# LSTM with attention: scores in groups of 64 keys, and the hidden part of the output made turned

## The chip, the cores and the metric

The kernel runs on one core of one Trainium2 chip. The metric is device time in microseconds (us). The kernel before took 5734.92 us (median of 3 runs, 5734.32 to 5736.79).

## The reference

The whole program is a small decoder of two layers: a linear recurrence, an LSTM with attention, a mixture of experts, an RWKV-7 scan, cross attention and a second mixture. The change touches the LSTM with attention, which runs 512 steps one after the other for 4 sequences, with 256 features and 512 source positions (keys) per sequence:

```python
def attend(h):
    q = h @ Wq.T
    scores = jnp.einsum('bc,bsc->bs', q, context)
    alpha = jax.nn.softmax(scores, axis=-1)
    ctx = jnp.einsum('bs,bsc->bc', alpha, context)
    return jnp.tanh(jnp.concatenate([ctx, h], axis=-1) @ Wout.T + b_out)

def step(carry, x_t):
    h, c, attn = carry
    inp = jnp.concatenate([x_t, attn], axis=-1)
    gates = inp @ W_ih.T + b_ih + h @ W_hh.T + b_hh
    i, f, g, o = jnp.split(gates, 4, axis=-1)
    c = jax.nn.sigmoid(f) * c + jax.nn.sigmoid(i) * jnp.tanh(g)
    h = jax.nn.sigmoid(o) * jnp.tanh(c)
    attn_out = attend(h)
    return (h, c, attn_out), attn_out
```

Every step needs the attention output of the step before, so the steps can't overlap.

## The kernel before

`prepare_phase` (L169) computes once, before the steps: the input's share of the gates (`xg_rows` in DRAM), the context folded with Wq (`keys`) and with the context half of Wout (`values`, bias included). With these a step needs only products of h with `keys`, of the softmax weights with `values`, and of h with `w_out_h`.

`attention_lstm_phase` (L663) holds the steps. Its loop body has two steps and runs 256 times. Each engine has its own program, written out by hand, and the engines meet at semaphores. All matmuls are fp32; the profile shows two records for each. TensorE is used in strips: its 128 output partitions are four strips of 32, and four matmuls, each with one strip, run side by side. In most places a strip is a sequence (batch) b; in `turn`, `select` and the gates it is one of the four quarters of a row of outputs.

One step, in PE's order (L922 to L958):

- `scores(c, k)` (L852): chunk c of 128 keys, half k of h. For each b, a window of 4 columns of `hid` is the stationary operand. h of b stands in column PAD + SPACE*b and the rest is zero, so the window that starts c columns earlier puts the scores of chunk c in row c of strip b. `part` 0 holds chunks 0 and 1, `part` 1 chunks 2 and 3, each a bank region of 128 columns. Half k = 0 can start when h[0] is there, k = 1 when h[1] is.
- DVE takes the maximum of a part (L1053), ACT the exp (L990). Parts have maxima of their own, and the differences are put right at the end by the `shrink` factors (L995, L1065 to L1077).
- `turn(part)` (L878): a matmul with columns of the identity as moving operand turns the exps so that keys lie on partitions; ACT copies them to `alpha` (L993).
- `hidden_part` (L862): h times `w_out_h`, h stationary (17 columns) and the weights moving, 6 matmuls of 128 or 64 columns, into rows of the `ctx` banks that the context leaves free. `hidden_sel` in `masks` picks those rows later.
- `half_hid(0, 0)`: part of the next gates. Then `context(c, n)` (L870): the alphas of chunk c times `values`, output piece n of three (128, 64 and 64 columns), each row of a strip a chunk. `turn(1)` lies among them.
- `select(o)` (L886): after ACT and DVE have copied the context to `out_row`, a matmul with `sel_scaled` (4 moving columns) adds up the rows of each sequence with their softmax factors, and the hidden rows with factor 1, and turns the result to feature-major. ACT takes tanh of it to `attn` (L1004).
- `gates`: `o_gate_x_hid`, then `half_attn` of both halves and `o_gate_attn`. DVE and ACT compute the cell and h from them (L1011 to L1030), while PE starts the next step's `half_x`.

`by_batch` picks every SPACE-th column, the four sequences; ROWS (13) is the number of stationary columns in the gates' matmuls.

Of the kernel before, what the change touches and what calls it, by code (L numbers as in the profile page):

```python
# [2 lines left out]

# [139 lines left out]
SPACE = 4  # L143
ROWS = SPACE * (BATCH - 1) + 1
PAD = SPACE
PARTS = 2
XROWS = TOK + UNROLL * BATCH


SEL, OWN_PART, HIDDEN_SEL, PLACE = 0, BATCH, BATCH + SC, 2 * BATCH + SC  # L150
MASKS = PLACE + ROWS
# [17 lines left out]
def prepare_phase(nc, d, g, xg_dram, w_attn, w_hid, w_out_h, keys, values, ident, masks):  # L169
# [5 lines left out]
    with Scope(nc) as s:  # L175
# [27 lines left out]
        KV_LOADS, GATES_LOADS = 4, 8  # L203
# [47 lines left out]
        def _(sp):  # L251
# [13 lines left out]
            sp.dma_start(ident[:, :], d["ident"]).then_inc(gates_loaded, 16)  # L265
# [397 lines left out]
def attention_lstm_phase(nc, d, g):  # L663
# [14 lines left out]
    with Scope(nc) as s:  # L678
# [5 lines left out]
        ident = s.sb("lstm_ident", [P, P])  # L684
        masks = s.sb("lstm_masks", [P, MASKS])

        prepare_phase(nc, d, g, xg_dram, w_attn, w_hid, w_out_h, keys, values, ident, masks)

        sel_batch = masks[:, SEL:SEL + BATCH]
        own_part = masks[:, OWN_PART:OWN_PART + SC]  # L690
        hidden_sel = masks[:, HIDDEN_SEL:HIDDEN_SEL + BATCH]
        place = masks[:, PLACE:PLACE + ROWS]
        with Scope(nc) as q:
# [11 lines left out]
            expo = q.sb("lstm_expo", [P, PARTS, P])  # L705
            alpha = q.sb("lstm_alpha", [P, BATCH, SC, 2 * SPACE - 1])
            spread_max = q.sb("lstm_spread_max", [P, 2 * (STRIP + 4)])
            spread_total = q.sb("lstm_spread_total", [P, 2 * (STRIP + 4)])
            neg_max_all = q.sb("lstm_neg_max_all", [P, 1])
            shrink = q.sb("lstm_shrink", [P, SC])  # L710
            weighed = q.sb("lstm_weighed", [P, SC])
            total_sum = q.sb("lstm_total_sum", [P, 1])
            own_terms = q.sb("lstm_own_terms", [P, SC])
# [10 lines left out]
            ctx_half = [0, 1, 1]  # L724
# [60 lines left out]
            def alpha_rows(part):  # L785
                return alpha[:, :, 2 * part:2 * part + 2, SPACE - 1]

            def turned_rows(part):
                return turned_ps[part].rearrange("p (b r) -> p b r", r=2)
# [19 lines left out]
            def _(pe):  # L809
# [42 lines left out]
                def scores(c, k):  # L852

                    part, n = c // 2, c % 2
                    for b in range(BATCH):
                        lo = PAD + SPACE * b - c
                        mm = pe.matmul(part_rows(score_ps[part], b), hid[:, k, lo:lo + SPACE],  # L857
                                       keys[:, k, b * SRC + c * P:b * SRC + (c + 1) * P],
                                       start=(n == 0 and k == 0), stop=(n == 1 and k == KC - 1))
                    return mm  # L860

                def hidden_part():  # L862

                    for k in range(KC):
                        for n, cols in enumerate(ctx_cols):
                            j = KC * k + ctx_half[n]
                            pe.matmul(ctx_ps[n][j * STRIP:j * STRIP + PAD + ROWS, :], hid[:, k, 0:PAD + ROWS],
                                      w_out_h[:, k, cols], start=True, stop=False)

                def context(c, n):  # L870

                    for b in range(BATCH):
                        mm = pe.matmul(part_rows(ctx_ps[n], b), alpha[:, b, c, SPACE - 1 - c:2 * SPACE - 1 - c],  # L873
                                       values[:, b * SC + c, ctx_cols[n]],
                                       start=(c == 0 and b % KC != ctx_half[n]), stop=(c == SC - 1))
# [1766 lines left out]
```

## Time and profile before

| | |
|---|---|
| median of 3 runs | 5734.92 us |
| profiled execution | 5734.24 us |
| its span | 5732.5 us |
| TensorE (PE) busy | 5209.2 us, 91% |
| VectorE (DVE) busy | 3553.1 us, 62% |
| ScalarE (ACT) busy | 1985.4 us, 35% |
| granted TensorE clock, mean | 0.968 |

Durations are read from the profiled execution. The span is the time from its first to its last instruction. The busy time of an engine is the time in which at least one of its instructions runs, so four matmuls side by side count once. The duration of one matmul record contains the fill and drain of the array; how closely matmuls follow each other is read from the starts. "PEld" is TensorE's loading of stationary operands. Each LSTM step looks like the others, so one step of the timeline stands for all.

### The profile page before, as it was taken

What the parts mean: (1) busy time and instruction counts of PE and PEld (TensorE: products, weight loads), DVE (VectorE), ACT (ScalarE), POOL (GpSimd) and SP (SyncE); (2) the same over time, 40 slices, a digit from 0 to 9 for tenths busy, and PEclk for the clock granted to TensorE, in tenths of its full rate; (3) what the DMA queues carried; (4) which work ended last, traced back from release to release, by engine and by line L of the source; (5) the groups of instructions that cost most, each with busy time, mean ns of one, the idle gap of its engine ahead of it and who ended that gap; (6) DMA issues with size and microseconds to landing.
All of it is one profiled execution on the core that took longest, in us unless ns stands there. A gap on an engine that the chain in (4) does not pass through costs nothing. (4 is left out here: it accounts for less than half of the span.)

```text
span 5732.5 us, 382651 instructions
## 1 busy us (share of the span) xinstructions
PE 5209.2 (91%) x171240; PEld 3824.2 (67%) x171240; DVE 3553.1 (62%) x15410; ACT 1985.4 (35%) x7977; POOL 345.7 (6%) x795
## 2 busy tenths in 40 slices
PE   9899999999999999999999999998688879797989
PEld 4677877877878778778778778776444434443433
DVE  5455555555555555555555555554798999999931
ACT  2244444444444444444444444442222222223221
POOL 0000000000000000000000000000111211212100
PEclk9999999999999999999999999999799889898999
DMA  2000000000000000000000000002111101010111
GB/s 99 35 2 2 2 2 2 2 2 2 2 2 2 2 2 2 2 2 2 2 2 2 2 2 2 2 2 86 45 54 39 44 16 54 25 54 25 57 36 54
DMA packets 45677, 111.60 MB, mean 19 GB/s; under 512 B 8192, under 2 KB 10240, under 8 KB 45072
## 3 DMA queue, kind: packets, MB, share of 16 engines
q1 hardware_dynamic: 44144, 109.39, 6.2%
q10 hardware_dynamic: 1440, 1.06, 0.1%
q8 instruction: 48, 0.79, 0.1%
q14 instruction: 45, 0.37, 0.0%
HBM read 99.90 MB, written 10.52 MB: 19 GB/s over the span
## 5 line engine op out<-in xcount | busy, mean ns | idle before, releaser
L857 PE MATMUL lstm_part_ps<-lstm_keys,lstm_hid 128*4 128x128 f32 x32768 | 1025.9, 273 | 207.1 <-DVE lstm_hid L1029 207.1
L857 PEld LDWEIGHTS lstm_part_ps<-lstm_keys,lstm_hid 128*4 128x4 f32 x32768 | 770.6, 86 | 431.5 <-DVE lstm_hid L1029 417.2
L873 PE MATMUL lstm_ctx_ps<-lstm_values,lstm_alpha 128*4 128x128 f32 (+1 forms) x49152 | 1041.2, 237 | 0.3 <-issue 0.3
L873 PEld LDWEIGHTS lstm_ctx_ps<-lstm_values,lstm_alpha 128*4 128x4 f32 x49152 | 905.6, 86 | 64.8 <-issue 0.5
L1053 DVE TENSOR_REDUCE lstm_neg_max<-lstm_part_ps 128x1 f32<-128x128 f32 x1024 | 299.2, 292 | 678.9 <-PE lstm_part_ps L857 678.9
L1011 DVE STREAM_TRANSPOSE lstm_gates<-lstm_half_ps 128x96 f32<-128x96 f32 x1026 | 290.6, 283 | 567.6 <-PE lstm_half_ps L816 543.8
L990 ACT ACTIVATE lstm_expo<-lstm_part_ps,lstm_neg_max 128x128 f32<-128x128 f32 x1024 | 376.4, 368 | 649.0 <-DVE lstm_neg_max L1053 649.0
L816 PE MATMUL lstm_half_ps<-lstm_w_hid,lstm_hid 128*13 128x96 f32 x16384 | 564.0, 245 | 0.0
L816 PE MATMUL lstm_half_ps<-lstm_w_attn,lstm_attn 128*13 128x96 f32 x16448 | 435.0, 246 | 1.6 <-issue 1.6
L2087 ACT ACTIVATE mix_gated<-mix_gate_ps 115x512 f32<-115x512 f32 (+2 forms) x200 | 112.6, 563 | 776.2 <-PE mix_gate_ps L1815 776.1
L816 PEld LDWEIGHTS lstm_half_ps<-lstm_w_hid,lstm_hid 128*13 128x13 f32 x16384 | 367.4, 94 | 0.0
L979 ACT ACTIVATE lstm_cell<-lstm_gates 128x12 f32<-128x12 f32 x1024 | 224.6, 219 | 411.1 <-DVE lstm_gates L1011 411.1
L1815 PE MATMUL mix_gate_ps<-xT,mix_ring 128*115 128x512 f32 (+3 forms) x800 | 363.8, 578 | 0.0
L1824 PE MATMUL mix_up_ps<-mix_xw,mix_ring 128*115 128x512 f32 (+2 forms) x704 | 320.7, 579 | 46.2 <-DVE mix_weighted L2391 37.4
L1844 PE MATMUL mix_down_ps<-mix_weighted,mix_ring 115*128 115x512 f32 (+3 forms) x800 | 358.4, 571 | 1.1 <-DVE mix_weighted L2391 1.0
L1094 POOL TENSOR_TENSOR xT<-xT,lstm_attn 128x8 f32 x512 | 105.2, 206 | 3636.2 <-ACT lstm_attn L1004 3636.2
L816 PEld LDWEIGHTS lstm_half_ps<-lstm_w_attn,lstm_attn 128*13 128x13 f32 x16448 | 302.6, 93 | 19.3 <-issue 2.0
L816 PE MATMUL lstm_half_ps<-lstm_xg,lstm_masks 128*13 128x96 f32 x8224 | 306.6, 250 | 8.7 <-DMA lstm_xg<-xg_rows 8.7
L993 ACT COPY lstm_alpha<-lstm_part_ps 128x8 f32<-128x8 f32 x1024 | 177.9, 174 | 377.7 <-PE lstm_part_ps L882 377.7
L2364 DVE TENSOR_TENSOR rw_terms<-rw_state,rw_sc 128x384 f32<-128x384 f32 x512 | 299.7, 585 | 6.7
L987 ACT ACTIVATE lstm_tanh_c<-lstm_cell 128x4 f32<-128x4 f32 x1024 | 210.7, 206 | 196.6 <-DVE lstm_cell L1022 154.6
L1029 DVE SCALAR_TENSOR_TENSOR lstm_hid<-lstm_o_col,lstm_tanh_c 128x4 f32<-128x4 f32 x1024 | 170.8, 167 | 174.0 <-ACT lstm_tanh_c L987 139.2
(324 smaller groups left out, 8196.2 us busy)
## 6 DMA issues: line engine op xcount, KB each, us to landing
mix_ring<-in_sm_chunks SPq DMA_DIRECT2D x120, 358.0 KB, 3.0
mix_ring<-in_mix_chunks SPq DMA_DIRECT2D x80, 384.0 KB, 3.1
lstm_xg<-xg_rows SPq DMA_DIRECT2D x514, 16.0 KB
xg_rows<-rec_lam SPq DMA_DIRECT2D x16, 512.0 KB, 2.6
xT<-in_xT SPq DMA_DIRECT2D x4, 512.0 KB, 8.7
ctxT<-in_ctxT SPq DMA_DIRECT2D x1, 2048.0 KB, 14.5
out_xT<-xT SPq DMA_DIRECT2D x4, 512.0 KB, 3.8
lstm_w_x<-in_lstm_w_x SPq DMA_DIRECT2D x1, 1024.0 KB, 17.2
```

The costliest lines, as they stand in the source:

```text
L816: mm = pe.matmul(ps[j * STRIP:j * STRIP + ROWS, :], rows, w[:, j * HID + cols.start:j * HID + cols.stop], start=start, stop=stop)
L857: mm = pe.matmul(part_rows(score_ps[part], b), hid[:, k, lo:lo + SPACE], keys[:, k, b * SRC + c * P:b * SRC + (c + 1) * P], start=(n == 0 ...
L873: mm = pe.matmul(part_rows(ctx_ps[n], b), alpha[:, b, c, SPACE - 1 - c:2 * SPACE - 1 - c], values[:, b * SC + c, ctx_cols[n]], start=(c == ...
L979: act.activation(cell[:, k, 0:GATES - 1, :], by_batch(turned), ACT.Tanh).then_inc(half_tanh[k], 1)
L987: act.activation(tanh_c[:, k, :], cell[:, k, GATES - 1, :], ACT.Tanh, scale=0.5).then_inc(c_tanh[k], 1)
L990: act.activation(expo[:, part, :], score_ps[part], ACT.Exp, bias=neg_max[:, part:part + 1]).then_inc(exp_ready, 1)
L1011: dve.transpose(gates[:, k, :], half_ps[k]).then_inc(half_turned[k], 1)
L1053: dve.tensor_reduce(neg_max[:, part:part + 1], score_ps[part], AX_X, ALU.max, negate=True)\
L1815: mm = pe.matmul(gate_ps[0:m, 0:width], ring[:, at, k * e:k * e + m], token_block(x, i)[:, k, :], start=(k == 0), stop=(k == KC - 1))
L1824: mm = pe.matmul(up_ps[0:m, 0:width], ring[:, at, lo:lo + m], xw[:, k, 0:width] if x.weighted(n) else token_block(x, i)[:, k, :], start=(k ...
L1844: mm = pe.matmul(down_ps[:, o_, 0:width], ring[0:m, gn % RING, lo + o_ * P:lo + (o_ + 1) * P], gw[0:m, gn % 2, 0:width], start=(n == 0), s ...
L2364: dve.tensor_tensor(terms[:, :, :, :], before.unsqueeze(1).to_broadcast([P, 3, HALF, HD]), sc[:, parity, UNIT_KEY:RECV + 1, t, :].unsqueez ...
```

## The change

SPACE becomes 8 and the 512 keys of a sequence are scored in 8 groups of 64 (`SUBS`, `SUB`). A part is now 4 groups: 4 rows of a strip, 64 columns. A window of `hid` has 8 columns instead of 4 and starts up to 7 columns earlier. The number of score matmuls doubles, from 32 to 64 a step, each with 64 moving columns instead of 128. The maximum, the exp and the sum of the exps run over 64 columns per part instead of 128.

`turn` writes 16 columns instead of 8: both halves of a 128-key chunk are brought back together, group 2*pair to partitions 0 to 63 and group 2*pair + 1 to partitions 64 to 127. Its moving operand is no longer the identity but 16 columns of `masks`, side by side, with zeros elsewhere. `alpha` takes two rows for each chunk, and the context's window moves by 2 a chunk. Softmax factors exist for 8 groups instead of 4.

`hidden_part` has operands exchanged: 32 columns of `w_out_h` are stationary, and four elements of h, 8 apart, are moving. There are 16 matmuls of 4 columns instead of 6 of 64 or 128. They write straight into `attn_ps`, and `select` accumulates on them (start=False). `hidden_sel` goes, so `sel_scaled` is a plain multiplication. `attn_ps[1]` gets a PSUM bank of its own, and `turned_ps[0]` moves to a context bank. ROWS becomes 25, by which the gates' matmuls have 25 stationary columns.

```diff
-SPACE = 4
+SUB = P // 2
+SUBS = SRC // SUB
+SPACE = SUBS
 ROWS = SPACE * (BATCH - 1) + 1
 PAD = SPACE
 PARTS = 2
+PART_SUBS = SUBS // PARTS
+TURNED = BATCH * PART_SUBS
...
-            expo = q.sb("lstm_expo", [P, PARTS, P])
-            alpha = q.sb("lstm_alpha", [P, BATCH, SC, 2 * SPACE - 1])
+            expo = q.sb("lstm_expo", [P, PARTS, SUB])
+            alpha = q.sb("lstm_alpha", [P, BATCH, SC, 2 * SPACE])
...
-            attn_ps = [part_ps[o][:, P:P + BATCH] for o in range(KC)]
-            score_ps = [part_ps[n][:, 0:P] for n in range(PARTS)]
-            turned_ps = [part_ps[n][:, 2 * P:2 * P + 2 * BATCH] for n in range(PARTS)]
+            attn_bank = q.ps("lstm_attn1_ps", [P, NB])
+            attn_ps = [part_ps[0][:, P:P + BATCH], attn_bank[:, 0:BATCH]]
+            score_ps = [part_ps[n][:, 0:SUB] for n in range(PARTS)]
+            turned_ps = [bank[:, 2 * P:2 * P + TURNED] for bank in (ctx_bank[KC], part_ps[1])]
...
             def alpha_rows(part):
-                return alpha[:, :, 2 * part:2 * part + 2, SPACE - 1]
+                return alpha[:, :, 2 * part:2 * part + 2, SPACE - 1:SPACE + 1]
...
                 def scores(c, k):
 
-                    part, n = c // 2, c % 2
+                    part, n = divmod(c, PART_SUBS)
                     for b in range(BATCH):
                         lo = PAD + SPACE * b - c
                         mm = pe.matmul(part_rows(score_ps[part], b), hid[:, k, lo:lo + SPACE],
-                                       keys[:, k, b * SRC + c * P:b * SRC + (c + 1) * P],
-                                       start=(n == 0 and k == 0), stop=(n == 1 and k == KC - 1))
+                                       keys[:, k, b * SRC + c * SUB:b * SRC + (c + 1) * SUB],
+                                       start=(n == 0 and k == 0), stop=(n == PART_SUBS - 1 and k == KC - 1))
                     return mm
 
+                def part_scores(part, k):
+
+                    for n in range(PART_SUBS):
+                        mm = scores(part * PART_SUBS + n, k)
+                    return mm
+
                 def hidden_part():
 
-                    for k in range(KC):
-                        for n, cols in enumerate(ctx_cols):
-                            j = KC * k + ctx_half[n]
-                            pe.matmul(ctx_ps[n][j * STRIP:j * STRIP + PAD + ROWS, :], hid[:, k, 0:PAD + ROWS],
-                                      w_out_h[:, k, cols], start=True, stop=False)
+                    for o in range(KC):
+                        for k in range(KC):
+                            for j in range(QUARTERS):
+                                lo = o * P + j * STRIP
+                                pe.matmul(attn_ps[o][j * STRIP:(j + 1) * STRIP, :], w_out_h[:, k, lo:lo + STRIP],
+                                          by_batch(hid[:, k, PAD:]), start=(k == 0), stop=False)
...
                 def turn(part):
 
-                    part_columns = ident[:, :].rearrange("p (b r) -> p b r", r=STRIP)[:, :, 2 * part:2 * part + 2]
                     for j in range(QUARTERS):
-                        mm = pe.matmul(turned_ps[part][j * STRIP:(j + 1) * STRIP, :], expo[:, part, j * STRIP:(j + 1) * STRIP],
-                                       part_columns, start=True, stop=True)
+                        half, lo = j // 2, j % 2 * STRIP
+                        col = TURN + (2 * part + half) * TURNED
+                        mm = pe.matmul(turned_ps[part][j * STRIP:(j + 1) * STRIP, :], expo[:, part, lo:lo + STRIP],
+                                       masks[:, col:col + TURNED], start=True, stop=True)
                     mm.then_inc(alpha_turned, 1)
...
                         mm = pe.matmul(attn_ps[o][j * STRIP:(j + 1) * STRIP, :], out_row[:, lo:lo + STRIP], sel_scaled[:, :],
-                                       start=True, stop=True)
+                                       start=False, stop=True)
...
                         pe.wait_ge(h_ready[0], t + 1)
-                        for c in (0, 1):
-                            scores(c, 0)
+                        part_scores(0, 0)
                         pe.wait_ge(h_ready[1], t + 1)
-                        scores(0, 1)
-                        scores(1, 1).then_inc(scores_ready, 1)
-                        for c in (2, 3):
-                            scores(c, 0)
-                        scores(2, 1)
-                        scores(3, 1).then_inc(scores_ready, 1)
+                        part_scores(0, 1).then_inc(scores_ready, 1)
+                        part_scores(1, 0)
+                        part_scores(1, 1).then_inc(scores_ready, 1)
...
-                        dve.scalar_tensor_tensor(out=sel_scaled[:, :], in0=sel_shrunk[:, :], scalar=inverse[:, 0:1],
-                                                 in1=hidden_sel, op0=ALU.mult, op1=ALU.add).then_inc(sel_ready, 1)
+                        dve.tensor_scalar(sel_scaled[:, :], sel_shrunk[:, :], inverse[:, 0:1], None, ALU.mult).then_inc(sel_ready, 1)
```

## Rows read from the trace of the kernel before

**Rows 1.** The page's first part: busy time, share of the span, instructions.

```profile
PE 5209.2 (91%) x171240; PEld 3824.2 (67%) x171240; DVE 3553.1 (62%) x15410; ACT 1985.4 (35%) x7977; POOL 345.7 (6%) x795
```

**Rows 2.** Windows: length, busy time and records of each engine, clock, DMA.

```profile
190.00:3800.00 3610.00, 3408.20 (x160264) 2882.02 (x160268) 1991.56 (x11376) 1475.47 (x6924) 101.54 (x494) 1.00 0.01 2
```

**Rows 3.** Timeline of one LSTM step: start us, length us, engine, line, operation.

```profile
2001.82 2.00 PE L857 MATMUL lstm_part_ps<-lstm_keys,lstm_hid 128*4 128x128 f32 x64 [0.41 <-DVE lstm_hid L1029]
...
2002.33 1.20 PEld L857 LDWEIGHTS lstm_part_ps<-lstm_keys,lstm_hid 128*4 128x4 f32 x48 [0.18 <-DVE lstm_hid L1029]
2003.02 0.29 DVE L1053 TENSOR_REDUCE lstm_neg_max<-lstm_part_ps 128x1 f32<-128x128 f32 x1 [0.74 <-PE lstm_part_ps L857]
2003.34 0.37 ACT L990 ACTIVATE lstm_expo<-lstm_part_ps,lstm_neg_max 128x128 f32<-128x128 f32 x1 [1.27 <-DVE lstm_neg_max L1053]
...
2003.76 0.25 PE L882 MATMUL lstm_part_ps<-lstm_ident,lstm_expo 128*32 128x8 f32 x8
...
2003.85 0.42 PE L867 MATMUL lstm_ctx_ps<-lstm_w_out_h,lstm_hid 128*17 128x128 f32 x12
2003.89 0.29 DVE L1053 TENSOR_REDUCE lstm_neg_max<-lstm_part_ps 128x1 f32<-128x128 f32 x1 [0.58 <-PE lstm_part_ps L857]
...
2004.06 0.37 PE L816 MATMUL lstm_half_ps<-lstm_w_hid,lstm_hid 128*13 128x96 f32 x8
2004.08 0.17 ACT L993 COPY lstm_alpha<-lstm_part_ps 128x8 f32<-128x8 f32 x1 [0.37 <-PE lstm_part_ps L882]
2004.22 0.37 ACT L990 ACTIVATE lstm_expo<-lstm_part_ps,lstm_neg_max 128x128 f32<-128x128 f32 x1
...
2004.30 0.51 PE L873 MATMUL lstm_ctx_ps<-lstm_values,lstm_alpha 128*4 128x128 f32 x16
...
2004.64 0.25 PE L882 MATMUL lstm_part_ps<-lstm_ident,lstm_expo 128*32 128x8 f32 x8
...
2004.72 1.62 PE L873 MATMUL lstm_ctx_ps<-lstm_values,lstm_alpha 128*4 128x64 f32 x80
...
2005.90 0.22 DVE L1077 SCALAR_TENSOR_TENSOR lstm_sel_scaled<-lstm_sel_shrunk,lstm_inverse,lstm_masks 128x4 f32<-128x4 f32 x1
2005.96 0.27 ACT L998 COPY lstm_out_row<-lstm_ctx_ps 128x128 f32<-128x128 f32 x1 [0.64 <-PE lstm_ctx_ps L873]
...
2006.15 0.51 PE L816 MATMUL lstm_half_ps<-lstm_w_hid,lstm_hid 128*13 128x96 f32 x16
...
2006.71 0.22 PE L890 MATMUL lstm_part_ps<-lstm_sel_scaled,lstm_out_row 128*32 128x4 f32 x8
...
2006.77 0.29 PE L816 MATMUL lstm_ctx_ps<-lstm_xg,lstm_masks 128*13 128x64 f32 x8
...
2007.10 0.84 PE L816 MATMUL lstm_half_ps<-lstm_w_attn,lstm_attn 128*13 128x96 f32 x32
...
2007.76 0.41 PE L816 MATMUL lstm_ctx_ps<-lstm_w_attn,lstm_attn 128*13 128x64 f32 x16
...
2009.11 0.62 PE L857 MATMUL lstm_part_ps<-lstm_keys,lstm_hid 128*4 128x128 f32 x16 [0.41 <-DVE lstm_hid L1029]
```

**Rows 4.** Waits of 1000 to 3500 us: total us, times, longest.

```profile
PEld lstm_part_ps L882 <- ACT lstm_expo L990: 79.4, 343, 0.2
```

**Rows 5.** Groups by line and form, 1000 to 3500 us: busy us, mean ns.

```profile
L1053 DVE TENSOR_REDUCE lstm_neg_max<-lstm_part_ps 128x1 f32<-128x128 f32 x686 | 200.5, 292 | 454.0 <-PE lstm_part_ps L857 454.0
...
L1061 DVE TENSOR_REDUCE lstm_total<-lstm_expo 128x2 f32<-128x256 f32 x343 | 144.0, 420 | 0.0
...
L998 ACT COPY lstm_out_row<-lstm_ctx_ps 128x128 f32<-128x128 f32 x343 | 91.4, 267 | 220.5 <-PE lstm_ctx_ps L873 220.5
...
L1000 ACT COPY lstm_out_row<-lstm_ctx_ps 128x64 f32<-128x64 f32 x343 | 73.0, 213 | 0.0
```

**Rows 6.** Instruction queue: packets, MB, share; whole span, then 190 to 3800 us.

```profile
q8 instruction: 48, 0.79, 0.1%
...
q8 instruction: 5, 0.08, 0.0%
```

More of the change, by code:

```diff
@@ L2 @@
 from contextlib import ExitStack
+import itertools
 import numpy as np
@@ L166, in sigmoid_columns, with prepare_phase @@
     return [halves_of(ap)[:, :, :, 0:2 * STRIP], quarters(ap)[:, :, KC * HALF_W:]]
-def prepare_phase(nc, d, g, xg_dram, w_attn, w_hid, w_out_h, keys, values, ident, masks):
+def prepare_phase(nc, d, g, xg_dram, w_attn, w_hid, w_out_h, keys, values, masks):
     QT = NB // QUARTERS
@@ L683, in attention_lstm_phase @@
         values = s.sb("lstm_values", [P, BATCH * SC, DIM])
-        ident = s.sb("lstm_ident", [P, P])
         masks = s.sb("lstm_masks", [P, MASKS])
-        prepare_phase(nc, d, g, xg_dram, w_attn, w_hid, w_out_h, keys, values, ident, masks)
+        prepare_phase(nc, d, g, xg_dram, w_attn, w_hid, w_out_h, keys, values, masks)
         sel_batch = masks[:, SEL:SEL + BATCH]
-        own_part = masks[:, OWN_PART:OWN_PART + SC]
-        hidden_sel = masks[:, HIDDEN_SEL:HIDDEN_SEL + BATCH]
+        own_part = masks[:, OWN_PART:OWN_PART + SUBS]
         place = masks[:, PLACE:PLACE + ROWS]
@@ L785, in alpha_rows @@
             def alpha_rows(part):
[L786 removed]
+                return alpha[:, :, 2 * part:2 * part + 2, SPACE - 1:SPACE + 1]
             def turned_rows(part):
[L789 removed]
+                return turned_ps[part].rearrange("p (b c h) -> p b c h", b=BATCH, h=2)
             @block.sync
@@ L870, in context @@
                 def context(c, n):
                     for b in range(BATCH):
-                        mm = pe.matmul(part_rows(ctx_ps[n], b), alpha[:, b, c, SPACE - 1 - c:2 * SPACE - 1 - c],
+                        mm = pe.matmul(part_rows(ctx_ps[n], b), alpha[:, b, c, SPACE - 1 - 2 * c:2 * SPACE - 1 - 2 * c],
                                        values[:, b * SC + c, ctx_cols[n]],
-                                       start=(c == 0 and b % KC != ctx_half[n]), stop=(c == SC - 1))
+                                       start=(c == 0), stop=(c == SC - 1))
@@ L1030, in new_hidden @@
                                              in1=tanh_c[:, k, :], op0=ALU.add, op1=ALU.mult).then_inc(h_ready[k], 1)
-                for ps in (*half_ps, *part_ps, *ctx_bank):
+                for ps in (*half_ps, *part_ps, *ctx_bank, attn_bank):
                     dve.memset(ps[:, :], 0.0)
@@ L2617, in laid_out @@
         masks[b * STRIP:b * STRIP + SPACE, SEL + b] = 1
-        for j in range(QUARTERS):
-            masks[j * STRIP + PAD + SPACE * b, HIDDEN_SEL + b] = 1
         masks[b, PLACE + SPACE * b] = 1
-    for c in range(SC):
+    for c in range(SUBS):
         masks[np.arange(QUARTERS) * STRIP + c, OWN_PART + c] = 1
+    for b, c in itertools.product(range(BATCH), range(SUBS)):
+        part, n = divmod(c, PART_SUBS)
+        pair, half = divmod(n, 2)
+        masks[b * STRIP + c, TURN + (2 * part + half) * TURNED + b * PART_SUBS + 2 * pair + half] = 1
     d["lstm_masks"] = masks
```

23 lines of the change are left out of this document (11 added, 12 removed).

## The prediction

> **What bounds the kernel now.** I read the busy shares first: TensorE (PE) is busy 91% of the span, DVE 62%, ACT 35% [rows 1]. Only the LSTM phase is edited, so next the view by stages: from 190 to 3800 us the clock is granted in full and PE is busy 3408 of 3610 us, 94% [rows 2]. The printed chain of waits follows only the phases behind the loop, so the bound has to be read from one step's timeline [rows 3]. Its first score matmul starts at 2001.82 and the next step's at 2009.11, so a step takes 7.29 us, and 512 of them 3732 us. Below, 3.76 means 2003.76.
>
> PE is in three states in a step. (a) From 1.82 it does 64 score records (32 fp32 matmuls, two records each). They are four concurrent streams, one per strip of 32 output partitions, so I count in rounds of four records. Part 0 is complete at 3.02, where DVE takes its maximum; ACT's exp runs 3.34 to 3.71, and PE's `turn(0)` starts at 3.76. PE ran out of scores before that: the wait of its weight loads at L882 for this exp is 79.4 us over 343 steps, 0.23 a step [rows 4]. (b) From 3.76 to 4.30 PE does `turn(0)`, `hidden_part`, `half_hid(0,0)` and then waits a little for `alpha`, which ACT copies out at 4.08 to 4.25. (c) From 4.30 to the end of the gates PE's rows follow each other without a gap; what it needs comes earlier than it asks: `sel_scaled` is done at 6.12 and `out_row` of piece 0 at 6.23, while the second `select` begins at 6.71. Behind the gates the cell update runs on DVE and ACT, untouched but for strides. So the step is one serial ring, and in (c) any shift of PE shifts the end by as much.
>
> **Prices in rounds** [rows 3]. 64 columns: L816 into ctx goes 6.77 to 7.10, 24 records, 0.33/6 = 0.055; I use 0.056. 96 columns: 7.10 to 7.76, 8 rounds, 0.0825. 128 columns: L873 x80 starts 4.72, its follower 6.15; 1.43 less 14 rounds of 0.056 leaves 0.108 for each of 6; I use 0.109. `select` (4 contiguous moving columns, 32-wide weights): 6.71 to 6.77 for two rounds, 0.03 each. `turn` (8 moving columns, taken in pairs 32 elements apart): 4.64 to 4.72, nearer 0.085 for two rounds with both turns read. So small matmuls with a broken-up moving operand cost about 0.085 a pair of rounds, contiguous ones 0.06.
> The Trainium skill (TensorE: Matmul & The Clock Gate, "Wait — 56ns, not 53.3ns?") says that start-to-start never drops under about 25 ns however small the matmul is. By that alone the 84 more records of a step would cost 2.1 us, some 1075 us in all. The trace disagrees where the records go to four strips: L882's eight records at 4.64 have all begun when the next line's begins at 4.72, some 10 ns each.
>
> **Part by part.**
> 1. *Scores in eight groups of 64 keys.* Records per step 64 to 128, each half as wide. From h[1] (weight load at 2.33) 12 rounds of 0.109 = 1.31 become 24 of 0.056 = 1.34: PE is free at 3.67 instead of 3.64. Before h[1]: 8 rounds of 0.056 = 0.45 in place of 0.44, and 0.51 are there (1.82 to 2.33), free. Part 0's last round starts 0.05 later and its matmul is 0.05 shorter, so part 0 is ready at 3.03, part 1's maximum starts at 3.93 instead of 3.89.
> 2. *Maximum over 64 columns.* 292 ns for 128 and 420 for 2x128 [rows 5]: 1.0 ns a column, 0.228 instead of 0.292, each part.
> 3. *Exp over 64 columns.* Copies by ACT take 267 ns for 128 columns, 213 for 64 [rows 5]: 0.054 less. Exp 0 ends at 3.71 + 0.01 - 0.064 - 0.054 = 3.60; `turn(0)` could start 0.05 later, 3.65, but PE is free at 3.67. It starts at 3.67, 0.09 earlier. What was PE's wait is now PE's own work. Exp 1 ends at 4.59 + 0.034 - 0.118 = 4.51.
> 4. *`turn`* has 16 contiguous moving columns from `masks` instead of 8 in pairs. Bounds are 0.06 and 0.085; I take 0.06, since the length is still far under 64 columns and it is contiguous like `select`'s. It is two rounds, so 0.025 saved, twice a step. ACT's copy grows by 8 columns, 0.007.
> 5. *`hidden_part`* turned: 6 matmuls become 16, 12 records 32, in 8 rounds. The moving operand is four elements of h, now 8 apart. Before: 3.85 to 4.06, 0.21. After, 4 pairs of rounds: 0.24 as `select`, 0.34 as `turn`, 0.45 at the price of 64 columns. I take 0.34, the nearest row with a broken-up moving operand. The Trainium skill (SBUF — State Buffer, "Door 1: The DMA port swizzle", its paragraph on cachelines) has a penalty for each access that crosses to a new 16-byte line; four elements 32 bytes apart are four lines, `turn`'s old pattern also four. `select`'s price against `turn`'s old one agrees with it, the rule points to 0.34 rather than 0.24.
> 6. *Where the context starts.* PE: 3.67 + 0.06 + 0.34 + `half_hid(0,0)` 0.165 = 4.23. `alpha[0]`: 0.54 from `turn(0)` to the context before (3.76 to 4.30), less 0.025 and more 0.007, gives 4.19. PE decides: 4.23 against 4.30. Up to `turn(1)` lie 2 x 0.109 + 2 x 0.056 = 0.33: 4.56, and exp 1 + 0.05 is 4.56 too, against 4.64. `turn(1)` gives 0.025 more. All of stage (c) is 0.095 earlier.
> 7. *`select` accumulates on the hidden part in PSUM, `sel_scaled` is a plain scaling.* Count and form of `select` stay, the DVE instruction is about as long (0.22) and has 0.5 us of slack; nothing. Own terms, shrink, weights over 8 instead of 4 columns: some ns each on a DVE chain that moves up by 0.08 with exp 1, hidden behind the contexts. Sum of exps: 0.13 shorter, also hidden. Weight loads of 8, 25 instead of 4, 13 columns: `turn` and `select` load 32 in rounds of 0.03, so every round of 0.056 or more covers them.
> 8. *Outside the loop*: one DMA less (the identity), larger masks, one more bank zeroed: 0 to 1 us once.
>
> Sum: 512 x 0.095 = 48.6 us less, 0.5 more. The profiled execution took 5734.24 us for a span of 5732.5; the median is 5734.92, 0.7 above, and I count from it: 5734.9 + 0.5 - 48.6 = 5686.8 us. Own range of this case: `turn` not cheaper (context at 4.255, 0.046 a step, 24 us) up to hidden at 0.24 (exp 1 decides; 0.109 a step, 56 us): 5680 to 5712.
>
> **Rivals.**
> *A. The turned hidden part costs as much as 64 columns or more* (0.056 a round). Its 0.45 put the context at 4.345 and `turn(1)` at 4.675; with 0.025 back the step is 0.01 longer: +5 us, 5740, no change, and slower if the price is higher still. For it: single elements 32 bytes apart are in no row. Against: the old `turn` broke its operand as often at less. Chance 0.09.
> *B. PE's instruction supply becomes the bound, slower.* No row shows rounds of 56 ns for long: 64-column runs last 6 rounds; the densest long stretch, 4.64 to 7.76, has 184 records in 3.12 us, 17.0 ns each, where the new scores ask for 14. If 17 is what the sequencer can feed, 96 records take 1.63, PE is free at 3.96, 0.29 later than in my sum, and the step is 0.2 longer: +100 us, 5837. It decides from about 15 ns a record. Against it: the 24 records from 6.77 and those just ahead of them come at 14 and less, and the 17.0 is fully explained by column counts. Chance 0.09.
> *C. The loop's code outgrows what PE holds.* From 190 to 3800 us the instruction queue moved 5 packets [rows 6]: the loop of two steps (1296 PE records) is fetched once and stays. The new one has 1632. If it doesn't stay, at least one packet is exposed at each of 256 jumps back. The whole span's 48 packets took 0.1% of 16 engines' time [rows 6], 92 us or 1.9 each, roughly: +490 us, 6180. Chance 0.04.
> The Trainium skill (Runtime: NRT & Kernel Launch, "Instruction fetch mechanics") gives PE room for 2048 instructions, by which 1632 stay; it also says that a jump outside two pages refetches, and five pages that are fetched once disagree with that.
> *D. The score part is better than summed* (the maximum or exp shrink more, rounds under 56 ns): 5672 or less. Chance 0.05.
>
> **How the numbers follow.** Forecast 0.73, A 0.09, B 0.09, C 0.04, D 0.05. The measurement tells 0.2%, 11.5 us, from no change. Faster: forecast and D and a little of A, 0.79; same 0.09; slower: B, C and a little of A, 0.12. The range 5670 to 5728 leaves out B, C, most of A and part of D.
>
> **What would show it.** A step of 7.195 us; PE's wait at L882 for exp 0 gone; 64-column score rounds of 56 ns; `turn(0)` 0.09 earlier; maxima near 228 ns and exps near 314; the 32 hidden records in about 0.34 us; no gap between `half_hid(0,0)` and the first context. Wrong: rounds of the scores over 60 ns (B), hidden records over 14 ns apart (A), instruction packets spread over the loop (C), or ACT's exp not shrinking, which would bring the wait at L882 back.

## The result, and the profile after

The changed kernel takes 7878.84 us (median of 4 runs, 7876.14 to 7893.32) against 5734.77 us: 1.3744 times as long, 95% interval 1.3727 to 1.3762. The forecast was 5687 us, with 5670 to 5728 as its range. Rival C, to which I gave 0.04, is what happened, and at more than four times the price I had put on it (2144 us over the kernel before, where I had 490).

The page of the changed kernel, its parts 1, 3 and 5:

```profile
PE 5708.2 (72%) x214248; PEld 4507.2 (57%) x214248; DVE 3418.8 (43%) x15411; ACT 1929.8 (24%) x7977; POOL 346.1 (4%) x795
...
q8 instruction: 1193, 19.55, 1.2%
...
L860 PE MATMUL lstm_part_ps<-lstm_keys,lstm_hid 128*8 128x64 f32 x65536 | 1370.2, 248 | 1083.5 <-issue 913.4
...
L1060 DVE TENSOR_REDUCE lstm_neg_max<-lstm_part_ps 128x1 f32<-128x64 f32 x1024 | 230.1, 225 | 1914.8 <-PE lstm_part_ps L860 1914.8
...
L997 ACT ACTIVATE lstm_expo<-lstm_part_ps,lstm_neg_max 128x64 f32<-128x64 f32 x1024 | 321.2, 314 | 1662.9 <-DVE lstm_neg_max L1060 1662.9
```

Two rows are as forecast: the maximum takes 225 ns (228 forecast, 292 in [rows 5]) and the exp 314 ns (314 forecast). Two are not: PE falls from 91% busy [rows 1] to 72%, and the instruction queue moves 1193 packets where it moved 48 [rows 6]. In front of the score matmuls PE is idle for 913 us with "issue" as the cause, which means that nothing in the profile was being waited for. On the page of the kernel before, the scores' line has 207.1 us of idle time ahead of it, all of it put down to DVE's `lstm_hid` and none to "issue".

PE's own timeline shows both faces of the changed loop (start, length; in brackets the idle time before and its cause):

```profile
2015.57 2.04 PE L860 MATMUL lstm_part_ps<-lstm_keys,lstm_hid 128*8 128x64 f32 x128 [0.39 <-DVE lstm_hid L1036]
2017.42 0.24 PE L893 MATMUL lstm_ctx_ps<-lstm_masks,lstm_expo 128*32 128x16 f32 x8
2017.48 0.29 PE L877 MATMUL lstm_part_ps<-lstm_hid,lstm_w_out_h 128*32 128x4 f32 x16
...
2017.80 0.38 PE L819 MATMUL lstm_half_ps<-lstm_w_hid,lstm_hid 128*25 128x96 f32 x7
2018.00 0.52 PE L883 MATMUL lstm_ctx_ps<-lstm_values,lstm_alpha 128*8 128x128 f32 x16
2018.34 0.23 PE L893 MATMUL lstm_part_ps<-lstm_masks,lstm_expo 128*32 128x16 f32 x8
2018.39 1.62 PE L883 MATMUL lstm_ctx_ps<-lstm_values,lstm_alpha 128*8 128x64 f32 x80
...
2020.78 0.85 PE L819 MATMUL lstm_half_ps<-lstm_w_attn,lstm_attn 128*25 128x96 f32 x32
...
2021.80 0.60 PE L819 MATMUL lstm_half_ps<-lstm_xg,lstm_masks 128*25 128x96 f32 x16
2026.66 1.03 PE L860 MATMUL lstm_part_ps<-lstm_keys,lstm_hid 128*8 128x64 f32 x29 [4.26 <-issue]
2030.19 2.10 PE L860 MATMUL lstm_part_ps<-lstm_keys,lstm_hid 128*8 128x64 f32 x72 [2.51 <-issue]
```

The step from 2015.57 is undisturbed: the gates' attention part begins 5.21 us after the first score matmul, where the kernel before needs 5.28 (7.10 - 1.82, [rows 3]). Then the loop jumps back and PE stands still for 4.26 us with nothing to wait for, does 29 records, and stands still for 2.51 us more. So the change does what it was meant to do where it can run, and something that isn't in any of its instructions costs 2171 us (7878.8 less the 5707.7 us of e2 below, whose loop is the same).

Over the loop, windows of the changed kernel and of e2 (length; busy time and records of PE, PEld, DVE, ACT, POOL; granted clock; DMA):

```profile
230.00:6000.00 5770.00, 3942.98 (x204558) 3588.71 (x204554) 1886.71 (x11535) 1441.67 (x7020) 102.45 (x501) 0.88 0.02 5
```

```profile
230.00:3800.00 3570.00, 3375.47 (x201560) 3114.85 (x201556) 1835.77 (x11362) 1438.19 (x6917) 100.81 (x494) 1.00 0.01 2
```

Brought to the same number of records (x 1.015), e2 needs 3623 us, 3426 of them busy. The changed kernel is busy 517 us longer and idle 1630 us longer. In its loop the granted clock is 0.88 in the mean, a mixture of stretches at 2.4 and at 1.2 GHz; in e2, which issues the same instructions without the pauses, it is 1.00. So the lower clock comes with the pauses, and it costs at most a quarter of the loss: 517 of 2147 us, in which longer busy time from work cut up by pauses is contained too.

### The profile page after: what moved, and what is told of

The parts are those of the page before. It is cut to its first block and busy times, and to the rows that moved or that the text cites. A ratio compares the mean times of both kernels' runs of the same rounds, so it can differ in the third digit from the quotient of the medians.

```text
span 7878.1 us, 468667 instructions
## 1 busy us (share of the span) xinstructions
PE 5708.2 (72%) x214248; PEld 4507.2 (57%) x214248; DVE 3418.8 (43%) x15411; ACT 1929.8 (24%) x7977; POOL 346.1 (4%) x795
## 3 DMA queue, kind: packets, MB, share of 16 engines
q8 instruction: 1193, 19.55, 1.2%
## 5 line engine op out<-in xcount | busy, mean ns | idle before, releaser
L860 PE MATMUL lstm_part_ps<-lstm_keys,lstm_hid 128*8 128x64 f32 x65536 | 1370.2, 248 | 1083.5 <-issue 913.4
L860 PEld LDWEIGHTS lstm_part_ps<-lstm_keys,lstm_hid 128*8 128x8 f32 x65536 | 1190.5, 103 | 1266.8 <-issue 998.3
L883 PE MATMUL lstm_ctx_ps<-lstm_values,lstm_alpha 128*8 128x128 f32 (+1 forms) x49152 | 1131.5, 245 | 163.9 <-issue 163.8
L883 PEld LDWEIGHTS lstm_ctx_ps<-lstm_values,lstm_alpha 128*8 128x8 f32 x49152 | 1023.4, 93 | 199.6 <-issue 180.3
L819 PE MATMUL lstm_half_ps<-lstm_w_hid,lstm_hid 128*25 128x96 f32 x16384 | 647.9, 254 | 122.3 <-issue 122.3
L997 ACT ACTIVATE lstm_expo<-lstm_part_ps,lstm_neg_max 128x64 f32<-128x64 f32 x1024 | 321.2, 314 | 1662.9 <-DVE lstm_neg_max L1060 1662.9
L819 PEld LDWEIGHTS lstm_half_ps<-lstm_w_hid,lstm_hid 128*25 128x25 f32 x16384 | 397.4, 107 | 147.7 <-issue 147.6
L819 PE MATMUL lstm_half_ps<-lstm_w_attn,lstm_attn 128*25 128x96 f32 x16448 | 444.1, 248 | 0.0
L819 PEld LDWEIGHTS lstm_half_ps<-lstm_w_attn,lstm_attn 128*25 128x25 f32 x16448 | 328.0, 103 | 6.3 <-issue 0.2
L819 PE MATMUL lstm_half_ps<-lstm_xg,lstm_masks 128*25 128x96 f32 x8224 | 302.5, 253 | 9.0 <-DVE lstm_attn L1044 9.0
```

What stands on the lines that cost most here:

```text
L819: mm = pe.matmul(ps[j * STRIP:j * STRIP + ROWS, :], rows, w[:, j * HID + cols.start:j * HID + cols.stop], start=start, stop=stop)
L997: act.activation(expo[:, part, :], score_ps[part], ACT.Exp, bias=neg_max[:, part:part + 1]).then_inc(exp_ready, 1)
```

## The experiments

**Theory A.** PE keeps a limited number of blocks of its instructions, and what counts is how many blocks the loop touches. **Theory B.** The number of instructions counts, wherever they begin. **Theory C.** The new instructions themselves (twice the score matmuls, the small turned ones) stall PE's sequencer. A block is what one packet of the instruction queue brings. The packets are 16 KB each (19.55 MB / 1193). The Trainium skill (Runtime: NRT & Kernel Launch, "Instruction fetch mechanics") says that they are blocks of 256 instructions and that PE's memory is 128 KiB, eight of them. In the built programs each fp32 matmul stands for four PE instructions, as the trace's two loads and two matmuls show. The loop before has 324 matmuls and 14 others: 1310 instructions, 5.1 blocks. The changed one has 408 and 14: 1646, 6.4 blocks. 1417 instructions stand ahead of both, 5.54 blocks. (The 14 and the 1417 were counted in the built programs; the traces bear them out in the main, with some 1360 loads and matmuls of PE ahead of the first score in either kernel.)

The loops and their places, in blocks counted in the built program (the true count is a little further on, see e6), with the instruction queue's packets in the whole span:

| kernel | loop | from | to | packets | us |
|---|---|---|---|---|---|
| before | 1310 | 5.54 | 10.65 | 48 | 5735 |
| changed | 1646 | 5.54 | 11.96 | 1193 | 7879 |
| e1, PE's loop of one step | some 830 | 5.54 | 8.8 | 46 | 5719 |
| e2, shifted by 140 | 1646 | 6.08 | 12.51 | 50 | 5708 |
| e3, shifted by 40 | 1646 | 5.69 | 12.12 | 2345 | 9866 |
| e4, before + turned hidden part | 1390 | 5.54 | 10.97 | 49 | 5735 |
| e5, shifted by 280 | 1646 | 6.63 | 13.06 | 1194 | 7765 |
| e6, shifted by 96 | 1646 | 5.91 | 12.34 | 50 | 5711 |
| e7, before, shifted by 100 | 1310 | 5.93 | 11.04 | 49 | 5736 |
| e8, e2 with loops of four on ACT and DVE | 1646 | 6.08 | 12.51 | 50 | 5712 |
| e9, changed without the hidden part | 1518 | 5.54 | 11.46 | 49 | 5707 |
| e10, before + 84 dummies in the loop | 1647 | 5.54 | 11.97 | 1193 | 8360 |
| e11, e10 shifted by 140 | 1647 | 6.08 | 12.52 | 50 | 7057 |

The traces of the runs that don't refetch test the count. Up to 300 us after the start, when every loop has gone round once, the queue has brought 10 packets in the kernel before, 8 in e1, 11 in e4, e7 and e9, and 12 in e2, e6, e8 and e11, and until the loop ends it brings no more. These are the numbers of the blocks in which the loops end, by the table and the small offset that e6 gives (block 0 is not among the packets). The size of a block shows as well. In the loop's first pass in e2 PE pauses where it enters a new block:

```profile
194.84 0.77 PE L860 MATMUL lstm_part_ps<-lstm_keys,lstm_hid 128*8 128x64 f32 x41 [0.81 <-issue]
...
198.64 1.32 PE L883 MATMUL lstm_ctx_ps<-lstm_values,lstm_alpha 128*8 128x128 f32 x63 [1.75 <-issue]
...
202.09 0.29 PE L819 MATMUL lstm_ctx_ps<-lstm_w_hid,lstm_hid 128*25 128x64 f32 x2 [1.05 <-issue]
```

Between the first and the second of these pauses it does 127 matmul records, between the second and the third 128. Each has its weight load, so that is 254 and 256 instructions.

**e1: PE's loop holds one step.** The input rows get one buffer in two pieces, so that nothing in PE's program depends on the parity of the step; the other engines keep loops of two.

```diff
-                with pe.Fori(0, SEQ // UNROLL) as i:
-                    for u in range(UNROLL):
-                        t = i * UNROLL + u
-                        nxt = (u + 1) % UNROLL
+                with pe.Fori(0, SEQ) as t:
+                    for u in (0,):
...
-                    sp.dma_start(xg[0:BATCH, u, :], xg_dram[bass.ds(t * BATCH, BATCH), :]).then_inc(xg_loaded[u], 16)
+                    sp.dma_start(quarters(xg[0:BATCH, :])[:, :, xg_cols[n]],
+                                 quarters(xg_dram[bass.ds(t * BATCH, BATCH), :])[:, :, xg_cols[n]]).then_inc(xg_loaded[n], 16)
```

> The changed kernel, with PE's loop holding one step instead of two (about 830 PE instructions in its body instead of 1646; 512 passes instead of 256). The work of a step is the same; the input rows have one buffer, loaded in two pieces. Theory (the loop's code no longer stays in PE's instruction memory): the instruction queue falls silent between 250 us and the end of the loop, the 'issue' gaps go, and the time is near 5700 us: the undisturbed step of the changed kernel, 7.16 us, with up to 0.14 us for 256 more jumps (36 us), so 5695 to 5740. Rival (the new small matmuls or the doubled number of score matmuls stall PE's sequencer, whatever the loop's length): the issue gaps stay with the work, the time stays over 7000 us.

5718.92 us (5717.4 to 5723.54), ratio to the kernel before 0.9975 (0.9965 to 0.9985), 46 packets. All the work of the change is in it and PE has as many records (214248), so theory C falls: no new instruction stalls by itself.

**e2 and e3: the same loop, moved.** Dummy matmuls run once, ahead of the loop.

```diff
+                for _ in range(35):
+                    pe.matmul(ctx_bank[KC][0:ROWS, NB - 1:NB], place, masks[:, 0:1], start=True, stop=True)
                 with pe.Fori(0, SEQ // UNROLL) as i:
```

> The changed kernel with 35 dummy matmuls of one column (140 PE instructions, 0.55 of a 256-instruction block) once ahead of the loop; the loop itself is untouched. Counted from PE's first instruction the changed loop begins at 5.5 blocks and ends at 11.96 or, with a few instructions of preamble, just over 12: eight blocks are touched. Shifted, it runs from 6.1 to 12.5: seven. Theory A (blocks touched decide, eight are too many, seven fit): the refetching stops, about 5700 us. Theory B (the number of instructions decides, 1646 are too many wherever they begin): as the changed kernel, 7880 us within 3%.

> As the one before with 10 dummy matmuls (40 instructions, 0.16 of a block): the loop then runs from 5.7 to 12.1 blocks, still eight. Both theory A and theory B expect about 7880 us (A because of eight blocks, B because of 1646 instructions). If it were fast, the dummies themselves would heal it or the counting of blocks is off by more than 0.1.

With 35 dummies 5707.69 us (5705.29 to 5710.49), ratio 0.9955 (0.9939 to 0.9972). With 10 dummies 9866.5 us (9856.73 to 9872.21), ratio 1.7207. The instruction queues of e2 and of e3 (packets, MB, share):

```profile
q8 instruction: 50, 0.82, 0.1%
```

```profile
q8 instruction: 2345, 38.42, 1.8%
```

The two programs differ by 100 instructions that run once, and by 4159 us. Theory B falls. Theory A holds, with one miss: e3 was expected at the changed kernel's 7880 us. In e3 each of the 256 passes fetches about nine blocks, (2345 - 50) / 256. In the changed kernel it is 4.5 a pass, and they come in every second one: its instruction queue moves nine packets from 2021 to 2052 us and none from 2052 to 2068, and from the first score matmul of one step to that of the next it takes 13.9 and 13.6 us (a refetched pass, from 2026.66 on) and then 7.2 and 11.6 us (a pass from memory, with the pause at the next jump back at its end). The starts of the four steps, and the queue from 2021 to 2052 us:

```profile
2026.66 1.03 PE L860 MATMUL lstm_part_ps<-lstm_keys,lstm_hid 128*8 128x64 f32 x29 [4.26 <-issue]
...
2040.51 0.28 PE L860 MATMUL lstm_part_ps<-lstm_keys,lstm_hid 128*8 128x64 f32 x2 [0.39 <-DVE lstm_hid L1036]
...
2054.13 2.04 PE L860 MATMUL lstm_part_ps<-lstm_keys,lstm_hid 128*8 128x64 f32 x128 [0.54 <-DVE lstm_hid L1036]
...
2061.36 2.04 PE L860 MATMUL lstm_part_ps<-lstm_keys,lstm_hid 128*8 128x64 f32 x128 [0.39 <-DVE lstm_hid L1036]
...
2072.94 1.03 PE L860 MATMUL lstm_part_ps<-lstm_keys,lstm_hid 128*8 128x64 f32 x29 [4.74 <-issue]
```

```profile
q8 instruction: 9, 0.15, 2.3%
```

A fetched block costs 4159 / 2295 = 1.8 us in e3 and 2171 / 1143 = 1.9 us in the changed kernel, the lower clock included.

**e5 and e6: shifts by 280 and 96 instructions**, 70 and 24 dummies.

> The changed kernel with 70 dummy matmuls (280 PE instructions, 1.09 blocks) once ahead of the loop. The loop then runs from block 6.63 to 13.06 and touches eight blocks again. Theory A (blocks touched decide): slow again, as the shift by 40 (9870 us, about nine blocks fetched in each pass of two steps). Rival (a longer stretch ahead of the loop is what healed it, or the shift by 140 was fast for another reason): as the shift by 140, 5708 us.

> The changed kernel with 24 dummy matmuls (96 PE instructions) ahead of the loop: from block 5.91 to 12.34, eight blocks, 24 instructions short of the boundary that the shift by 140 passed. Theory A: slow, 9870 us. If the blocks are counted from a place over 24 instructions further on, or the limit is another, it is fast, 5708 us.

e5: 7764.92 us, ratio 1.3542 (1.3515 to 1.3569), 1194 packets. More ahead of the loop does not heal it; it is the place in the block that counts, and 280 is 24 modulo 256. (The expectation named the slower of the two slow forms, and the milder came; what separates them lies between a shift of 24 and one of 40, and I did not look further.) e6: 5711.17 us, ratio 0.9958 (0.9942 to 0.9973), against the expectation of theory A. Its last sentence is what holds: the true count starts at least 23 instructions (0.09 of a block) further on, since the loop of e6 must begin at 6.0 or behind it, and at most 78 (0.30), since e3's must not. This offset was fitted to e6 and e3 after their results. The first pauses in e2 give it independently: the first of them comes after 87 score records, 174 instructions, and if block 7 begins there, the offset is some 60 (an estimate: 1792 less 1557 and 174, and a few waits less). With 23 to 78 the changed loop ends at 12.06 to 12.27 and touches blocks 5 to 12, eight; e3, e5 and e10 touch eight; e2, e4, e6, e8, e9 and e11 touch seven; the kernel before and e7 touch six and e1 four. All eight-block loops refetch and no other does.

**e4: only the turned hidden part**, on the kernel before, with what belongs to it (a bank for `attn_ps[1]`, `turned_ps[0]` in a context bank, `select` accumulating, `sel_scaled` a plain scaling).

```diff
...
-                            pe.matmul(ctx_ps[n][j * STRIP:j * STRIP + PAD + ROWS, :], hid[:, k, 0:PAD + ROWS],
-                                      w_out_h[:, k, cols], start=True, stop=False)
+                                pe.matmul(attn_ps[o][j * STRIP:(j + 1) * STRIP, :], w_out_h[:, k, lo:lo + STRIP],
+                                          by_batch(hid[:, k, PAD:]), start=(k == 0), stop=False)
...
```

> The kernel before with only the hidden part turned and accumulated under the selection (16 matmuls of 4 columns for 6; scores in groups of 128 as before, 4 rows of a strip). The loop has 1390 PE instructions and ends at about 11.0 blocks. Both theories of instruction supply: no refetching. Its own price: the 32 records take 0.32 us as in the changed kernel's undisturbed step instead of 0.21; PE then comes to the context at 3.76 + 0.085 + 0.32 + 0.165 = 4.33 instead of 4.30: +0.03 us a step, 5750 us (5735 to 5760). If the new small matmuls themselves stalled the sequencer, it would be slower by hundreds of us.

5735.26 us (5731.06 to 5742.33), ratio 1.0006 (0.9997 to 1.0016): no change, where +0.03 us a step was expected. Its timeline:

```profile
2002.92 2.00 PE L858 MATMUL lstm_part_ps<-lstm_keys,lstm_hid 128*4 128x128 f32 x64 [0.40 <-DVE lstm_hid L1031]
2004.87 0.25 PE L884 MATMUL lstm_ctx_ps<-lstm_ident,lstm_expo 128*32 128x8 f32 x8
2004.95 0.29 PE L869 MATMUL lstm_part_ps<-lstm_hid,lstm_w_out_h 128*32 128x4 f32 x16
...
2005.20 0.25 PE L817 MATMUL lstm_half_ps<-lstm_w_hid,lstm_hid 128*13 128x96 f32 x1
...
2005.22 0.37 PE L817 MATMUL lstm_half_ps<-lstm_w_hid,lstm_hid 128*13 128x96 f32 x7
2005.41 0.52 PE L875 MATMUL lstm_ctx_ps<-lstm_values,lstm_alpha 128*4 128x128 f32 x16
```

The 32 records take 4.95 to 5.20, 0.25 us instead of 0.21, and the context still starts 2.49 us after the first score (2.48 before, [rows 3]): they fit under the wait for ACT's copy. Here the moving elements of h stand 4 apart; in e2, where they stand 8 apart, the same 32 records take 0.29 us. So e4 shows that the exchange of operands costs nothing, but not the price at the changed kernel's spacing; that is read from e2 and e9.

**e7: the kernel before with 25 dummies ahead of its loop.**

> The kernel before with 25 dummy matmuls (100 PE instructions) ahead of its loop: 1310 instructions from block 5.93 to 11.04, seven blocks instead of six. Theory A (seven fit): no change, 5733 us within 0.2%, and no packets in the instruction queue during the loop. If six blocks (96 KB) were the limit, it would be slow by thousands of us; if the dummies had an effect of their own on a fitting loop, it shows here.

5736.16 us, ratio 1.0003 (0.9994 to 1.0013). The dummies have no effect of their own. With the offset found in e6 this loop touches blocks 6 to 11, six and not seven, so it says nothing on seven; that is shown by e2, e4, e6 and e9.

**e8: loops of four steps on ACT and DVE**, on e2.

```diff
-                with dve.Fori(0, SEQ // UNROLL) as i:
-                    for u in range(UNROLL):
-                        t = i * UNROLL + u
+                with dve.Fori(0, SEQ // 4) as i:
+                    for u in range(4):
+                        t = i * 4 + u
...
```

> The shift by 140, and the loops of ACT and DVE hold four steps instead of two (PE's still two). In the kernel before and in the shift by 140 every second step is 0.14 us longer (7.22 and 7.36; 7.16 and 7.30), and with PE's loop of one step that pattern stayed (7.18, 7.33), so the 0.14 us belongs to the jump of ACT or DVE. If so, 128 jumps fewer give 128 x 0.14 = 18 us: 5690. If the jump is not theirs: 5708.

5711.99 us, ratio 0.9963 (0.9949 to 0.9977): nothing gained. My reading was wrong. I had taken the steps' times from POOL's one instruction per step, and its pattern of 7.16 and 7.31 stayed with ACT and DVE jumping half as often. From first score matmul to first score matmul the step is 7.23 us throughout, so it is POOL's instruction alone that comes 0.07 us late in every second step. Its own jump back is the likely cause; no run tests that.

**e9: the changed kernel without `hidden_part`** (the attention output lacks the product of h with `w_out_h`, and `select` begins its sums itself), and with nothing ahead of the loop.

```diff
-                                       start=False, stop=True)
+                                       start=True, stop=True)
...
                         turn(0)
-                        hidden_part()
                         half_hid(0, 0)
```

> The changed kernel without the product of h with w_out_h (16 matmuls a step; the attention output lacks that part), and nothing ahead of the loop. The loop has 1518 PE instructions and ends at 11.5 blocks, and a shift of the count by the 24 to 79 instructions that the runs so far allow leaves it under 12: seven blocks. Theory A (blocks touched): no refetching, and 5708 us or a little less without any shift. Rival (the changed loop stalls for what its matmuls are, the shift being a coincidence): still over 7000 us. For the price of the turned hidden part: in the shift by 140 the first context waits for ACT's copy by 0.05 us, so that only what exceeds that cover is saved at the first context (nothing), and the step stays at 7.23 us: 5700 to 5708. If the hidden part were on the path, up to 0.3 us a step would go: 5560.

5706.55 us (5705.31 to 5710.43), ratio 0.995 (0.9934 to 0.9967), 49 packets. 128 instructions fewer in the loop, and it fits without a shift. PE's timeline:

```profile
2004.34 2.04 PE L860 MATMUL lstm_part_ps<-lstm_keys,lstm_hid 128*8 128x64 f32 x128 [0.40 <-DVE lstm_hid L1035]
2006.20 0.24 PE L893 MATMUL lstm_ctx_ps<-lstm_masks,lstm_expo 128*32 128x16 f32 x8
2006.27 0.35 PE L819 MATMUL lstm_half_ps<-lstm_w_hid,lstm_hid 128*25 128x96 f32 x8
2006.78 0.52 PE L883 MATMUL lstm_ctx_ps<-lstm_values,lstm_alpha 128*8 128x128 f32 x16 [0.17 <-ACT lstm_alpha L999]
```

Without the hidden part PE waits 0.17 us for `alpha`, and the context starts 2.44 us after the first score, as with it (2.43 in e2). The turned hidden part costs nothing here; rival A is answered.

**e10 and e11: the kernel before, made as long.** 42 dummies in each step, and in e11 35 more ahead of the loop.

```diff
+                        for _ in range(42):
+                            pe.matmul(ctx_bank[KC][0:ROWS, NB - 1:NB], place, masks[:, 0:1], start=True, stop=True)
                         pe.wait_ge(h_ready[0], t + 1)
```

> The kernel before, with 42 dummy matmuls of one column in each step ahead of the wait for h, so that its loop has 1647 PE instructions, one more than the changed one's, at the same place in the stream. None of the change is in it. Theory A: it refetches as the changed kernel does, 1100 to 2300 packets, and takes 7900 us or more (7879 plus the dummies' own price of 0.2 us a step over PE's idle 0.4 us, 100 us). Rival (the change's own instructions stall): 5735 to 5850.

> The one before with 35 more dummies once ahead of the loop (140 instructions): seven blocks. Theory A: no refetching; 5735 plus 0.2 us a step for the dummies, 5840 (5735 to 5950). Rival (too many instructions in the loop wherever they begin): as the one before.

e10: 8359.9 us, ratio 1.4578 (1.4546 to 1.4609); e11: 7057.39 us, ratio 1.2306 (1.2282 to 1.2331), two runs each. The queues of e10 and e11:

```profile
q8 instruction: 1193, 19.55, 1.0%
```

```profile
q8 instruction: 50, 0.82, 0.0%
```

Without a line of the change, a loop of 1647 instructions in the same place fetches exactly as many packets as the changed kernel, and the shift ends it. A packet costs less here than in the changed kernel, (8359.9 - 7057.4) / 1143 = 1.1 us. The time of e11 is 1200 us above what I expected, because I priced the dummies wrongly. From e11:

```profile
2008.54 2.21 PE L925 MATMUL lstm_ctx_ps<-lstm_masks 128*13 128x1 f32 x83
2010.60 0.34 PE L857 MATMUL lstm_part_ps<-lstm_keys,lstm_hid 128*4 128x128 f32 x3
```

83 records of one column, all in the same strip, take 2.06 us, 25 ns each, where I had reckoned 7 ns from records that go to four strips. The clock is lower too: 0.77 granted in the mean of the 7.29 us from 2000 (part at 2.4, part at 1.2 GHz), in which PE was never idle, where the kernel before has 1.00 and idle time in every step.

## Why the prediction was wrong

*The failed step* is the bound on the loop's code in rival C: "it is fetched once and stays. The new one has 1632", with 2048 as the room and 0.04 as the chance. I compared numbers of instructions. The runs showed in its place that the number of blocks that the loop touches decides: eight blocks refetch (1193 packets, 7879 us), seven stay (50 packets, 5708 us in e2). That needs the loop's place in PE's stream, which can be counted from the program: 5.54 to 11.96 with an uncertain offset, thus seven or eight blocks, at the edge. The packets in [rows 6] did not support the bound either: the five of the loop's first pass, with the block in which it begins, showed that six blocks stay, and said nothing on seven or eight. With that, 0.04 was too low.

*The price of C* was one packet exposed at each jump, 490 us. e3 shows what a loop that doesn't stay costs: about nine blocks are fetched in each pass and each leaves about 1.8 us exposed, 4159 us; in the changed kernel that happens in every second pass, 2171 us. The number of packets was wrong by 4.5 times. That the 1.9 us per packet came out is luck. It was worked out from a share rounded to 0.1%, which allows 1.0 to 2.9, and as the time that a packet takes; by the changed kernel's page a packet takes some 1.3 us (1.2% of 16 x 7878 us over 1193). What is exposed is something else: in the refetched pass from 2021 to 2052 us the nine packets come over 31 us, about 3.4 us each, while PE works through a block in 2.2 us when nothing is fetched (14.46 us for 6.43 blocks in e2). A reserve of one block read ahead of the loop's end, pushing out its first, would explain the nine packets for eight blocks and why eight don't stay; the runs fit it but don't show it. Why the passes alternate stays open.

*The steps of the likeliest case* can be read in e2, where nothing refetches. Its timeline:

```profile
2014.91 2.04 PE L860 MATMUL lstm_part_ps<-lstm_keys,lstm_hid 128*8 128x64 f32 x128 [0.39 <-DVE lstm_hid L1038]
...
2016.12 0.23 DVE L1062 TENSOR_REDUCE lstm_neg_max<-lstm_part_ps 128x1 f32<-128x64 f32 x1 [0.76 <-PE lstm_part_ps L860]
2016.38 0.31 ACT L999 ACTIVATE lstm_expo<-lstm_part_ps,lstm_neg_max 128x64 f32<-128x64 f32 x1 [1.21 <-DVE lstm_neg_max L1062]
2016.76 0.24 PE L893 MATMUL lstm_ctx_ps<-lstm_masks,lstm_expo 128*32 128x16 f32 x8
2016.83 0.29 PE L877 MATMUL lstm_part_ps<-lstm_hid,lstm_w_out_h 128*32 128x4 f32 x16
...
2017.10 0.19 ACT L1002 COPY lstm_alpha<-lstm_ctx_ps 128x16 f32<-128x16 f32 x1 [0.41 <-PE lstm_ctx_ps L893]
...
2017.12 0.26 PE L819 MATMUL lstm_half_ps<-lstm_w_hid,lstm_hid 128*25 128x96 f32 x1
...
2017.14 0.38 PE L819 MATMUL lstm_half_ps<-lstm_w_hid,lstm_hid 128*25 128x96 f32 x7
2017.34 0.52 PE L883 MATMUL lstm_ctx_ps<-lstm_values,lstm_alpha 128*8 128x128 f32 x16
...
2017.67 0.23 PE L893 MATMUL lstm_part_ps<-lstm_masks,lstm_expo 128*32 128x16 f32 x8
...
2017.73 1.62 PE L883 MATMUL lstm_ctx_ps<-lstm_values,lstm_alpha 128*8 128x64 f32 x80
...
2020.12 0.85 PE L819 MATMUL lstm_half_ps<-lstm_w_attn,lstm_attn 128*25 128x96 f32 x32
```

In us after the step's first score matmul:

| | before [rows 3] | predicted | e2 |
|---|---|---|---|
| `turn(0)` | 1.94 | 1.85 | 1.85 |
| first context | 2.48 | 2.41 | 2.43 |
| `turn(1)` | 2.82 | 2.74 | 2.76 |
| contexts behind it | 2.90 | 2.80 | 2.82 |
| `half_attn` | 5.28 | 5.18 | 5.21 |

- Scores, maximum and exp (steps 1 to 3) were right: 1.85. PE's wait for exp 0 is gone; the 32 rounds of scores take 1.85 us, 58 ns each, so rival B, by which a round would take 68 ns, is refuted.
- `turn` (step 4) is the term of the likeliest case that was mis-sized. PE leaves it after 0.06 to 0.07 as taken (16.76 to 16.83, 17.67 to 17.73), but its result comes no sooner. ACT's copy starts 0.34 after it (0.32 before) and takes 0.19 (0.17), where I had 0.295 and 0.18. So the context can start 0.58 after `turn(0)`, not 0.52, and that, not PE, decides when it starts: without the hidden part (e9) it starts no sooner. That is the 0.02 missing there, and it stays.
- The hidden part (step 5) takes 0.29 (16.83 to 17.12; 0.34 taken) and is covered (e9).
- The step comes to 7.23 us instead of 7.195, and the whole to 25 us less (5732.7 to 5707.7, medians measured side by side), not 48. Of the 0.09 us gained in front of `turn(0)`, ACT's copy takes some 0.03 back; the dummies ahead of e2's loop cost some 2 us once (35 x 4 instructions, 1.76 us from 190.83).

## What to carry to other kernels

- When a change lengthens an unrolled loop, count the instructions of the engine that has most, each fp32 matmul as four on PE, find the place of the loop in that engine's stream, and count the 256-instruction blocks that it touches: seven stayed on PE here, eight did not. The instruction queue's packets in the profile say at once which it is; what it brings in the loop's first pass shows in which block the loop ends.
- If a changed kernel is slow with "issue" gaps on one engine while others have nothing to show, look at that queue before anything else. Shifting the loop by a few dozen instructions, or giving that one engine a shorter loop, separates the change's worth (25 us here) from the price of its length (2171 us). The shorter loop (e1, 11 us slower than e2) touches four blocks, or five, wherever its start comes to lie, and so stays clear of the edge.

## What the runs showed of the hardware that I had not expected

- 100 PE instructions that run once, ahead of a loop, changed the time from 9866 to 5708 us.
- Between all and nothing there is a stable alternation: one pass from memory, the next refetched (4.5 packets a pass, 7879 us).
- A refetched loop gets its blocks one by one, with 1.8 to 1.9 us exposed for each (1.1 in e10). It is not the jump back alone that exposes them: the loop's first pass in e2, code run through for the first time, has the same pauses, of 0.29 to 1.82 us, with seven packets from 192 to 216 us. In the program's tail, from 3900 to 5700 us, e2 gets 38 packets, one in 47 us; there the costliest matmuls of PE have 512 columns and a block lasts that long. So what seems to count is how fast PE gets through a block; no run varied it alone.
- The same 32 records of the hidden part take 0.25 us with the moving elements of h 4 apart (e4) and 0.29 us with 8 apart (e2).
- Start-to-start of tiny matmuls is 25 ns in one strip and some 10 ns over four strips (e11 against L882 in [rows 3]). The rows differ in operands too, so that the strips are the reason is argued and not shown. The Trainium skill (TensorE: Matmul & The Clock Gate, "Wait — 56ns, not 53.3ns?") gives 25 ns without that distinction; e11 agrees with it for one strip.
